# A language-model tower on one core: a sum of heads turned the other way, steps moved between engines, a last stage reordered

## The chip, the core and the metric

The kernel runs on one core of a Trainium2 chip. Five engines work side by side, each through its own instructions in the order in which they are written: TensorE (PE in the profile; its weight loads are PEld), VectorE (DVE), ScalarE (ACT), GpSimd (POOL) and SyncE (SP), which here mostly starts transfers. They wait for one another by semaphores. The metric is the device time of one execution in microseconds (us), the median of the runs shown.

## What is computed

32 sequences of 96 token numbers pass through three parts. In short:

```
# 1: embedding and an additive attention
x = emb[tokens]*sqrt(128) + pe
q, k, v = x@Wq+bq, x@Wk+bk, x@Wv+bv
s[b,i,j] = sum_d a[d] * tanh(q[b,i,d] + k[b,j,d])
x = layer_norm(x + softmax(s)@v@Wo + bo); h = layer_norm(x + relu(x@W1+bf1)@W2 + bf2)
# 2: causal attention with 8 heads of 128
h = h + attn(layernorm(h))
# 3: 64 experts, two for each token, and a shared one
t = _ln(layernorm(h)); idx, w = two largest of softmax(t@Wr@codebook.T/0.7), scaled to sum 1
hmoe = sum_k w_k*(silu(t@W1[e_k]+b1)@W2[e_k]+b2) + 0.25*(silu(t@Ws1+bs1)@Ws2+bs2)
out = h + (x3 + hmoe + silu(_ln(hmoe)@Wf1+bf1)@Wf2+bf2)      # x3 = layernorm(h)
```

The tanh is taken of 32 x 96 x 96 x 128 sums, 37.7 million: most of the first part's work.

## The kernel before, in words

**The tower.** Two sequences make a pair (192 tokens); 16 pairs. The program is written as rounds n = -1 to 21. Each engine has a `body(n)`, a list by hand of the steps of a round; `at(n, k, step)` runs the step for pair n - k if there is one, so in a full round some six pairs are in work, each in another part. `at_end` holds a step until the last pair. Nothing but this order and the semaphores decides what runs when.

The costly part is the tanh: for a pair VectorE forms eight blocks of sums with `add` (L941, 128x2304 each), ScalarE takes `tanh` of each (L688), TensorE weights and sums each with `score` (L1385, 24 instructions of 192 columns). The rest is fitted between. `x_rows` (VectorE, L954) forms a pair's embedding rows scaled plus `pe_rows`; `xs_turn`, `qk` and `queries` (L932) follow and allow the first `add` of that pair; `keep_x` (GpSimd, L555) keeps the rows with a bias. The layer norms (`stats`, `means`, `variance` on VectorE, `root` on GpSimd, L568 and L573) come four times in a pair: x1, x2, h0 and h1. `variance` adds eps; `root` raises to the power -1/2.

**Attention 2.** For a pair: `heads_g` (TensorE, L1498, 8 heads, 192 columns each), `scores` (L1519), `mask_max` and `exp2`, `inv_sums`, `normalise` (GpSimd, L578), `pr_turn` (L1526), `heads_m` (L1505, the probabilities times the rows: a mean for each head), `mean_copy` (ScalarE). Then the heads' sum: `o_begin` lays the residual h0 into PSUM as [96 tokens, 2 x 128], and four blocks of `attend2` (L1539) add the heads: the mean is the weight operand (96 columns), `vo` moves (128 columns), 8 instructions a block. `h1_stats` reads the sum. Then routing: `tn_turn`, `logits`, `route`, `chosen`, `one_hot` (VectorE, L1107: which of 64 experts), `both_hot`, `ranks` (L1560, L1118: the row's place at its expert), and `scatter_rows` (GpSimd, L620): four indirect DMAs put a pair's rows to their experts in DRAM. `cum_pair` (L595) carries the counts on; in the list it stands behind the scatters.

**The drain.** After the last pair has its scores, the rounds go on with fewer pairs until it is routed. Blocks of the shared expert (`shared1`, `shared2`, L1572 and L1589) are placed there. When all is counted, TensorE forms the rows for each expert (L1651, the "count"), a chain of small steps makes the tables, and the expert stage begins: 81 tiles of 128 rows, about 163 us, each with two products of TensorE.

**The last stage.** 12 blocks of 256 tokens. VectorE: `mixture` (weighted expert results into `hm`, statistics, variance, and the residual `rh` = hm + x), then it waits for GpSimd's root (L675), forms `fn` (L1349), and adds the `output` of block j - 2 (L1358). TensorE turns fn (L1743) and does two products (L1751, L1764), with ScalarE between.

## Time and profile before

| | us |
|---|---|
| median of 3 runs | 800.54 (799.36 to 802.94) |
| the profiled execution | 801.53 |
| its span in the trace | 799.5 |
| TensorE busy | 743.0 |
| VectorE busy | 611.6 |
| ScalarE busy | 615.2 |
| GpSimd busy | 366.5 |

By stage: start 0 to 12.6, where the first `add` begins; the filling of the pipeline to 88; the full rounds 88 to 490; the drain to 564; the expert stage 572 to 735; the last stage 747 to 799.5. A row of the timeline gives start, length, engine, line, operation, and in brackets the idle time before and what ended it. A float32 product of TensorE stands as two instructions in the trace. The chain of waits is followed back from the last instruction, each step to what released it.

### The profile page before, as it was taken

To read this page: it belongs to the slowest core of one execution; us is meant where nothing else is said; L and a number is where in the kernel's file an instruction comes from. 1 tells how busy PE (TensorE), PEld (TensorE's weight loads), DVE (VectorE), ACT (ScalarE), POOL (GpSimd) and SP (SyncE) were. 2 spreads that over 40 slices of the span, in tenths; PEclk is the share of its full clock that TensorE was granted. 3 is DMA by queue.
4 is the path that set the end of the run, shared out by engine and by line. 5 is a ranking of instruction groups with operands and counts; after the bars stand their busy time and mean duration, and the time that the engine had idled before them with its cause. 6 is when DMAs were issued, how large, how long until landed. Compare 5 with 4: busy or idle time off the path is not lost.

```text
span 799.5 us, 21390 instructions
## 1 busy us (share of the span) xinstructions
PE 743.0 (93%) x7238; PEld 594.1 (74%) x7238; DVE 611.6 (76%) x1634; ACT 615.2 (77%) x1455; POOL 366.5 (46%) x482
## 2 busy tenths in 40 slices
PE   2767999999999999999999999986899899999898
PEld 1454776776777777777777777765799899998787
DVE  4999899999999999999999996533434345433785
ACT  2787899999999999999999998763356465655454
POOL 3211234456465465465465455766047355554121
PEclk9999899999999999999999999997999999999999
DMA  2950000000000000000000000001599999993501
GB/s 79 251 120 6 5 5 7 12 17 14 12 16 14 12 16 17 12 16 17 12 17 16 12 12 12 17 20 31 175 384 375 402 395 365 346 359 119 168 29 39
DMA packets 50096, 78.99 MB, mean 99 GB/s; under 512 B 7428, under 2 KB 34203, under 8 KB 50000
## 3 DMA queue, kind: packets, MB, share of 16 engines
q1 hardware_dynamic: 33824, 65.01, 23.8%
q0 software_dynamic: 5664, 7.92, 3.7%
q10 hardware_dynamic: 10512, 4.83, 2.2%
q8 instruction: 56, 0.92, 0.5%
q14 instruction: 40, 0.33, 0.1%
HBM read 63.95 MB, written 15.92 MB: 100 GB/s over the span
## 4 chain that ended last, share of the span: by engine, by line
PE 75%; DVE 6%; issue 4%; SPq 4%; DMA 3%; ACT 2%; POOL 2%; POOLq 0%; DVEq 0%; ACTq 0%
PE b_s L1385 15%; PE b_o L1539 7%; PE big L1695 6%; PE big L1498 6%; PE big L1505 5%; PE big L1519 5%; DVE arena L941 4%; PE b_y L1482 3%; PE b_qk L1706 3%; PE b_s L1706 3%; PE big L1526 3%; PE big L1751 3%; DMA arena<-in_wpack 3%; PE big L1470 3%; PE b_s L1764 2%
## 5 line engine op out<-in xcount | busy, mean ns | idle before, releaser
L941 DVE TENSOR_TENSOR arena<-qT,b_qk 128x2304 f32<-128x2304 f32 x128 | 323.9, 2536 | 0.1
L688 ACT ACTIVATE arena<-arena 128x2304 f32<-128x2304 f32 x128 | 275.6, 2156 | 17.6 <-DVE arena L941 17.6
L1385 PE MATMUL b_s<-arena,apad 128*32 128x192 f32 x3072 | 155.7, 339 | 9.1 <-ACT arena L688 9.0
L1385 PEld LDWEIGHTS b_s<-arena,apad 128*32 128x32 f32 x3072 | 89.4, 112 | 78.6 <-issue 29.1
L849 ACT ACTIVATE act_h<-big,arena 128x128 f32<-128x128 f32 x324 | 92.4, 368 | 71.5 <-PE big L1695 71.5
L656 POOL DMA_INDIRECT eo_dram<-gT,toff x81 | 79.7, 984 | 95.0 <-DVE gT L1270 91.3
L1695 PE MATMUL big<-hbT,arena 128*128 128x128 f32 x648 | 87.0, 278 | 5.3 <-DMA arena<-in_wpack 3.9
L578 POOL TENSOR_TENSOR kept<-kept,rs 96x384 f32<-96x384 f32 x64 | 52.8, 824 | 78.1 <-DVE rs L1077 77.7
L750 ACT ACTIVATE kept<-big,mx 96x96 f32<-96x96 f32 x256 | 83.6, 354 | 1.7 <-DVE mx L1071 1.5
L1695 PEld LDWEIGHTS big<-hbT,arena 128*128 128x128 f32 x648 | 79.6, 193 | 6.2 <-issue 5.5
L1259 DVE TENSOR_SCALAR hbT<-b_t,cols 128x128 f32<-128x128 f32 x81 | 33.2, 409 | 61.5 <-PE b_t L1688 61.5
L620 POOL DMA_INDIRECT rows_dram<-rows_now,slots x64 | 62.2, 971 | 16.7 <-issue 15.7
L1539 PE MATMUL b_o<-kept,vv 128*96 128x128 f32 x512 | 66.4, 274 | 0.0
L1539 PEld LDWEIGHTS b_o<-kept,vv 128*96 128x96 f32 x512 | 59.2, 163 | 5.7 <-issue 5.3
L750 ACT ACTIVATION_READ_ACCUMULATOR kept<-big,mx 96x1 f32 x256 | 57.0, 222 | 0.0
L1505 PE MATMUL big<-prT,vv 96*128 96x384 f32 x128 | 53.7, 501 | 0.0
L1519 PE MATMUL big<-gT,xaT 128*96 128x384 f32 x128 | 52.4, 490 | 0.6 <-ACT gT L734 0.6
L1498 PE MATMUL big<-xaT,kept 128*128 128x192 f32 x256 | 52.4, 340 | 0.0
L1071 DVE TENSOR_REDUCE mx<-big 96x4 f32<-96x384 f32 x64 | 35.1, 549 | 15.1 <-PE big L1519 15.1
L1498 PEld LDWEIGHTS big<-xaT,kept 128*128 128x128 f32 x256 | 42.6, 195 | 5.1 <-issue 4.6
L555 POOL TENSOR_TENSOR res<-xs,v_bias 96x256 f32<-96x256 f32 x16 | 11.7, 730 | 72.5 <-DVE xs L954 58.2
L1706 PE MATMUL b_s<-arena,act_h 128*128 128x128 f32 x328 | 43.4, 275 | 0.3 <-ACT act_h L849 0.3
(226 smaller groups left out, 1441.8 us busy)
## 6 DMA issues: line engine op xcount, KB each, us to landing
arena<-in_wpack SPq DMA_DIRECT2D x81, 578.0 KB, 9.1
prT<-rows_dram ACTq DMA_DIRECT2D x73, 64.5 KB
rows_dram<-act_h SPq DMA_DIRECT2D x1, 4128.0 KB, 24.1
arena<-eo_dram SPq DMA_DIRECT2D x4, 512.0 KB, 7.1
x_dram<-res SPq DMA_DIRECT2D x16, 96.0 KB, 1.7
out<-of SPq DMA_DIRECT2D x12, 128.0 KB, 1.8
eo_dram<-gT,toff POOLq DMA_INDIRECT x81, 5.6
rows_dram<-rows_now,slots POOLq DMA_INDIRECT x64, 2.3
```

Source lines behind the costliest of these rows:

```text
L656: pool.indirect_dma_start(eo_dram, bass.IndirectOffsetOnAxis(ap=toff[:, r:r + 1].bitcast(U32), axis=0), eo[r], None, bounds_check=TOPK * T ...
L688: act.activation(v, v, ACT.Tanh).then_inc(s["tanh"], 1)
L750: last = act.activation(pr[:, h, :], bank(p, f"scores {k}")[0:N, j * N:(j + 1) * N], ACT.Exp, bias=mx2[:, h:h + 1], scale=-1.0, accum_out= ...
L849: last = act.activation(act_h[:, i, c * TILE:(c + 1) * TILE], big[i][:, c * TILE:(c + 1) * TILE], ACT.Silu, bias=wslot[:, slot, 2 * DFF + ...
L941: dve.tensor_tensor(ring[c % TRING].rearrange("p (x m n) -> p x m n", m=CQ, n=N), qv.unsqueeze(3).to_broadcast([D, SPLIT * QG, CQ, N]), kv ...
L1385: last = pe.matmul(b_s[32 * a:32 * a + 32, 0:SPLIT * N], apad[:, 31 - line:63 - line], t[:, :, a, m, :], start=(line == 0), stop=(line == ...
L1498: last = pe.matmul(dst[:, j * TN:(j + 1) * TN], mh[:, h * D:(h + 1) * D], xaT[:, :], start=True, stop=True)
L1505: pe.matmul(dst[:, 0:4 * N], xa[p % 2][:, k // 2, :], prT[:, 4 * k:4 * k + 4, :].rearrange("p a n -> p (a n)"), start=True, stop=True).the ...
L1519: pe.matmul(dst[0:N, 0:4 * N], xaT[:, g * N:(g + 1) * N], gT[:, h:h + 4, g * N:(g + 1) * N], start=False, stop=True).then_inc(s["s2"], 1)
L1539: last = pe.matmul(p_o[:, g, :], meanT[:, g * H + h, :], vo[:, h * D:(h + 1) * D], start=False, stop=(k == 3 and h == H - 1))
L1695: last = pe.matmul(big[of_ring(t, 2)][:, c * TILE:(c + 1) * TILE], wslot[:, slot, c * D:(c + 1) * D], hbT[:, of_ring(t, 2), :], start=True ...
L1706: last = pe.matmul([b_s, b_qk][of_ring(t, 2)][:, 0:D], act_h[:, of_ring(t, 2), c * TILE:(c + 1) * TILE], wslot[:, slot, DFF + c * D:DFF + ...
```

## The change

- **The heads' sum is turned.** `vo` becomes the weight operand (128 columns) and the means of both sequences move (192 columns): eight products, in two `attend2` halves of four heads, into `p_oT`, [128, 192]. VectorE copies it to `oT` (`oT_copy`), and `o_rows` lays h0 and two products with the identity, which turn it back, into `p_o`. `h1_stats` waits for that. The blocks of `scores` and `heads_m` are numbered anew, so that a half has the same four heads of both sequences. `o_begin` goes; h0 gets a second buffer.
- **To GpSimd go** `x_rows` (as a multiplication and an addition), the additions of eps (now in `root` and `roots_h1`), and `one_hot` (as four comparisons).
- **The orders of all engines are new.** On GpSimd `root h0` stands behind `root x2`, `x_rows` and the first scatters, and `cum_pair` ahead of the scatters. On TensorE `shared1 1` and `shared1 2`, `shared2 0` and `shared2 1` stand in the last round, behind the last pair's `ranks` of the round before.
- **In the last stage** GpSimd forms the residual (`last_residual`, ahead of the root), `hm` gets a second buffer, `rh` a fourth, and `output(j - 2)` stands ahead of `f_rows(j)`, the step that forms fn.
- Some semaphores are merged; the order of ScalarE's list is new as well, its steps are the same.

The diff, cut to its core (of VectorE's list the new order, of TensorE's list the new order with the lines that stay):

```diff
-RESIDUALS = 3
+RESIDUALS = 4
...
-        hm = sb("hm", [128, G, D])
+        hm = [sb(f"hm_{i}", [128, G, D]) for i in range(2)]
...
-        h0 = sb("h0", [N, G, D])
+        h0 = [sb(f"h0_{i}", [N, G, D]) for i in range(2)]
...
+        p_oT = b_o[:, G * D:G * D + TN]
...
+            def x_rows(p):
+                wait(pool, s["xs_t"], p)
+                if p < EARLY:
+                    pool.wait_ge(s[f"emb{p}"], 16 * G)
+                else:
+                    pool.wait_ge(s["emb2"], 16 * G * (p - (EARLY - 1)))
+                if p == 0:
+                    pool.wait_ge(s["ld_a"], 16 * 5)
+                wait(pool, s["kept"], p)
+                pool.tensor_scalar(xs[:, :, :], pair_of(res, p) if p < EARLY else emb[:, :, :],
+                                   float(np.float32(D) ** np.float32(0.5)), None, ALU.mult).then_inc(s["scaled"], 1)
+                pool.wait_ge(s["scaled"], p + 1)
+                pool.tensor_tensor(xs[:, :, :], xs[:, :, :], pe_rows[:, :].unsqueeze(1).to_broadcast([N, G, D]),
+                                   ALU.add).then_inc(s["xs"], 1)
+
...
             def root(p, n):
                 pool.wait_ge(s["var_" + n], p + 1)
+                pool.tensor_scalar(ve[n][:, :], mv[n][:, :, 1], EPS if n == "h0" else EPS_TOK, None, ALU.add)\
+                    .then_inc(s["ve_" + n], 1)
+                pool.wait_ge(s["ve_" + n], p + 1)
                 pool.tensor_tensor(rstd[n][:, :], ve[n][:, :], halves[:, 0:G], ALU.pow)\
                     .then_inc(s["rstd_" + n], 1)
             def roots_h1(p):
+                wait(pool, s["shift"], p)
                 pool.wait_ge(s["var_h1"], p + 1)
+                pool.tensor_scalar(ve_h[:, 0:G], mv["h1"][:, :, 1], EPS, None, ALU.add)
+                pool.tensor_scalar(ve_h[:, G:3 * G].rearrange("p (a g) -> p a g", g=G),
+                                   mv["h1"][:, :, 1].unsqueeze(1).to_broadcast([N, 2, G]),
+                                   1.0 + EPS, EPS * EPS, ALU.mult, ALU.add).then_inc(s["ve_h1"], 1)
+                pool.wait_ge(s["ve_h1"], p + 1)
                 pool.tensor_tensor(rstd_h[:, :], ve_h[:, :], halves[:, :], ALU.pow).then_inc(s["rstd_h1"], 1)
...
+            def one_hot(p):
+                wait(pool, s["slot"], p)
+                pool.wait_ge(s["topf"], p + 1)
+                for g in range(G):
+                    for k in range(TOPK):
+                        j = g * TOPK + k
+                        last = pool.tensor_scalar(oh[:, g, k, :], iota_e[0:N, :], of_pair(topf, p)[:, j:j + 1], None,
+                                                  ALU.is_equal)
+                last.then_inc(s["hot"], 1)
...
             def body(n):
+                at(n, 6, one_hot)
+                at(n, 6, both_hot)
+                at(n, 0, gather_emb, 0)
+                at(n, 3, root, "x1")
+                at(n, 6, counted)
+                at(n, 4, setup)
+                at(n, 6, keep_rows)
+                at(n, 6, residual)
+                at(n, 0, gather_emb, 1)
+                at(n, 4, normalise, 0)
+                at(n, 6, cum_pair)
+                at(n, 3, x1_bias)
+                at(n, 5, roots_h1)
+                at(n, 4, normalise, 1)
+                at(n, 1, keep_x)
+                at(n, 4, normalise, 2)
+                at(n, 4, normalise, 3)
+                at(n, 3, root, "x2")
+                at(n, 0, x_rows)
                 at(n, 6, scatter_rows, 0)
-                at(n, 0, gather_emb, 0)
-                at(n, 3, root, "x2")
-                at(n, 0, gather_emb, 1)
-                at(n, 4, normalise, 1)
-                at(n, 4, normalise, 2)
                 at(n, 3, root, "h0")
-                at(n, 4, normalise, 3)
                 at(n, 6, scatter_rows, 1)
-                at(n, 6, cum_pair)
-                at(n, 0, keep_x)
-                at(n, 2, root, "x1")
-                at(n, 5, both_hot)
-                at(n, 0, setup)
-                at(n, 5, counted)
-                at(n, 5, residual)
-                at(n, 2, x1_bias)
-                at(n, 5, keep_rows)
-                at(n, 3, normalise, 0)
-                at(n, 4, roots_h1)
...
+            def last_residual(j):
+                pool.wait_ge(s["mixed"], j + 1)
+                if j >= RESIDUALS:
+                    pool.wait_ge(s["of"], j - RESIDUALS + 1)
+                pool.tensor_tensor(rh[j % RESIDUALS], hm[j % 2][:, :, :],
+                                   xr[:, j, :].rearrange("p (g d) -> p g d", g=G), ALU.add).then_inc(s["rh"], 1)
+
...
+                last_residual(j)
...
-            def x_rows(p):
-                wait(dve, s["xs_t"], p)
-                wait(dve, s["kept"], p)
-                if p < EARLY:
-                    dve.wait_ge(s[f"emb{p}"], 16 * G)
-                else:
-                    dve.wait_ge(s["emb2"], 16 * G * (p - (EARLY - 1)))
-                dve.scalar_tensor_tensor(xs[:, :, :], pair_of(res, p) if p < EARLY else emb[:, :, :],
-                                         float(np.float32(D) ** np.float32(0.5)),
-                                         pe_rows[:, :].unsqueeze(1).to_broadcast([N, G, D]),
-                                         ALU.mult, ALU.add).then_inc(s["xs"], 1)
-
...
+                last.then_inc(s["var_" + n], 1)
+
...
+            def oT_copy(p):
+                wait(dve, s["o_rows"], p)
+                dve.wait_ge(s["att2"], 2 * p + 2)
+                dve.tensor_copy(oT[:, :], p_oT).then_inc(s["oT"], 1)
+
...
+                at(n, 0, add, 2)
+                at(n, 3, inv_sums, 2)
+                at(n, 4, h1_shift)
+                at(n, 2, x2_stats)
+                at(n, 1, softmax1_max)
+                at(n, 3, inv_sums, 3)
+                at(n, 2, means, "x2")
+                at(n, 0, add, 3)
+                at(n, 2, x2_rows)
+                at_end(n, 5, shared_rows, 0)
+                at(n, 1, p1T_copy)
+                at(n, 2, x2_norm)
+                at(n, 2, h0_stats)
+                at(n, 1, x1_sums)
+                at(n, 2, means, "h0")
+                at(n, 1, x1_rows)
+                at(n, 0, add, 4)
+                at(n, 1, x1_stats)
+                at(n, 2, xa_norm)
+                at(n, 4, route)
+                at(n, 0, add, 5)
+                at(n, 4, chosen)
+                at(n, 1, means, "x1")
+                at(n, 0, setup)
+                at(n, 0, add, 6)
+                at(n, 3, oT_copy)
+                at(n, 0, add, 7)
+                at(n, 2, mask_max, 0)
+                at(n, 1, x1_norm)
+                at(n, 4, ranks)
+                at(n, -1, queries)
+                at(n, 2, mask_max, 1)
+                at(n, 2, inv_sums, 0)
+                at(n, -1, add, 0)
+                at(n, 3, h1_stats)
+                at(n, -1, add, 1)
+                at_end(n, 5, shared_rows, 1)
+                at(n, 3, means, "h1")
+                at(n, 2, mask_max, 2)
+                at(n, 2, inv_sums, 1)
+                at(n, 2, mask_max, 3)
...
+                if j >= 2:
+                    dve.wait_ge(s["rh"], j - 1)
...
-                ch.link(dve.tensor_tensor(rh[j % RESIDUALS], hm[:, :, :], xr[:, j, :].rearrange("p (g d) -> p g d", g=G),
-                                          ALU.add))
+
...
+            def output(j):
+                dve.wait_ge(s["rh"], j + 1)
+                dve.wait_ge(s["f2"], j + 1)
+                if j:
+                    dve.wait_ge(s["out"], 16 * j)
+                for g in range(G):
+                    last = dve.tensor_tensor(of[:, g, :], [b_s, b_qk][g][:, 0:D], rh[j % RESIDUALS][:, g, :], ALU.add)
+                last.then_inc(s["of"], 1)
+
+            for j in range(NB):
+                mixture(j)
...
                 if j >= 2:
                     output(j - 2)
-            ch.wait()
+                f_rows(j)
...
-                pe.matmul(dst[:, 0:4 * N], xa[p % 2][:, k // 2, :],
+                pe.matmul(dst[:, 0:4 * N], xa[p % 2][:, k % 2, :],
...
-                g = k // 2
-                h = (k % 2) * 4
+                pe.wait_ge(*big_read(p, f"heads_g {2 * (k // 2)}"))
+                pe.wait_ge(*big_read(p, f"heads_g {2 * (k // 2) + 1}"))
+                g = k % 2
+                h = (k // 2) * 4
...
+            def attend2(p, half):
+                if half == 0:
+                    wait(pe, s["o_rows"], p)
+                for g in range(G):
+                    pe.wait_ge(*big_read(p, f"heads_m {G * half + g}"))
+                of_heads = meanT[:, half * G * 4:(half + 1) * G * 4, :].rearrange("p (g a) n -> p a g n", g=G)
+                for j in range(4):
+                    h = 4 * half + j
+                    last = pe.matmul(p_oT, vo[:, h * D:(h + 1) * D], of_heads[:, j, :, :],
+                                     start=(h == 0), stop=(h == H - 1))
+                last.then_inc(s["att2"], 1)
+
+            def o_rows(p):
                 wait(pe, s["tn"], p)
-                pe.wait_ge(s["h0_rows"], p + 1)
-                pe.matmul(b_o[0:N, 0:G * D], ident[0:N, 0:N], h0[:, :, :].rearrange("p g d -> p (g d)"),
-                          start=True, stop=False).then_inc(s["o_init"], 1)
-
-            def attend2(p, k):
-                pe.wait_ge(*big_read(p, f"heads_m {k}"))
-                g = k // 2
-                for h in range((k % 2) * 4, (k % 2) * 4 + 4):
-                    last = pe.matmul(p_o[:, g, :], meanT[:, g * H + h, :], vo[:, h * D:(h + 1) * D],
-                                     start=False, stop=(k == 3 and h == H - 1))
-                last.then_inc(s["att2"], 1)
+                pe.wait_ge(s["oT"], p + 1)
+                pe.matmul(b_o[0:N, 0:G * D], ident[0:N, 0:N], h0[p % 2][:, :, :].rearrange("p g d -> p (g d)"),
+                          start=True, stop=False)
+                for g in range(G):
+                    last = pe.matmul(p_o[:, g, :], oT[:, g * N:(g + 1) * N], ident[:, :], start=False, stop=(g == G - 1))
+                last.then_inc(s["o_rows"], 1)
...
             def body(n):
+                at(n, 3, ffn1, 1)
+                at(n, 2, score, 6)
+                at(n, 4, scores, 2)
+                at(n, 4, scores, 3)
+                at(n, 3, ffn2)
+                at_end(n, 6, shared2, 0)
+                at(n, 2, score, 7)
                 at(n, 4, pr_turn, 0)
+                at(n, 4, pr_turn, 1)
+                at(n, 4, pr_turn, 2)
+                at(n, 2, products)
+                at(n, 4, heads_m, 0)
                 at(n, 2, p1_turn)
+                at(n, 4, pr_turn, 3)
+                at_end(n, 5, shared1, 0)
+                at(n, 4, heads_m, 1)
                 at(n, 1, score, 0)
                 at(n, 2, attend1)
+                at(n, 5, tn_turn)
+                at(n, 1, setup)
+                at_end(n, 6, shared1, 1)
                 at(n, 1, score, 1)
+                at(n, 4, heads_m, 2)
+                at(n, 4, heads_m, 3)
+                at(n, 5, logits)
+                at(n, 4, attend2, 0)
                 at(n, 1, score, 2)
+                at(n, 3, xa_turn)
+                at(n, 1, v_rows)
+                at(n, 4, attend2, 1)
+                at(n, 1, score, 3)
+                at(n, 3, heads_g, 0)
+                at(n, 0, xs_turn)
                 at_end(n, 6, shared2, 1)
                 at(n, 3, heads_g, 1)
                 at(n, 3, heads_g, 2)
+                at(n, 1, score, 4)
+                at(n, 3, scores, 0)
+                at(n, 5, ranks)
+                at(n, 3, heads_g, 3)
+                at(n, 0, qk)
+                at(n, 3, scores, 1)
                 at(n, 2, x1_turn)
+                at(n, 4, o_rows)
+                at(n, 1, score, 5)
+                at_end(n, 6, shared1, 2)
                 at(n, 2, ffn1, 0)
```

## Rows read from the trace of the kernel before

**Rows 1.** Busy by stretch: length; PE, PEld, DVE, ACT, POOL; granted clock; DMA.
```profile
241.59:272.14 30.55, 30.55 (x338) 22.30 (x342) 30.45 (x73) 29.82 (x66) 16.90 (x23) 1.00 0.06 15
541.00:560.00 19.00, 12.75 (x59) 10.35 (x58) 6.83 (x45) 5.84 (x12) 12.06 (x17) 0.71 0.12 32
```

**Rows 2.** Chain of waits in a round: start, us, engine, tile, line, instructions.
```profile
292.40 0.88 PE b_o L1539 x8
...
296.49 1.33 PE big L1498 x8
```

**Rows 3.** Timeline of the start: start, us, engine, line, operation, out<-in, [idle before].
```profile
8.81 0.42 DVE L954 SCALAR_TENSOR_TENSOR xs<-res,pe_rows 96x256 f32<-96x256 f32 x1 [3.21 <-DMA res<-in_L_tok_emb,eidx]
...
10.39 0.97 POOL L539 MEMSET act_h<- 128x1024 f32 x1
...
12.56 12.41 DVE L941 TENSOR_TENSOR arena<-qT,b_qk 128x2304 f32<-128x2304 f32 x5
```

**Rows 4.** Timeline of VectorE: `queries` at both ends of twelve rounds.
```profile
87.45 0.42 DVE L932 TENSOR_SCALAR qT<-b_qk,bqk 128x192 f32<-128x192 f32 x1 [0.17 <-PE b_qk L1408]
...
454.60 0.40 DVE L932 TENSOR_SCALAR qT<-b_qk,bqk 128x192 f32<-128x192 f32 x1
```

**Rows 5.** Timeline of the drain.
```profile
540.71 1.06 PE L1539 MATMUL b_o<-kept,vv 128*96 128x128 f32 x8
...
541.88 0.48 DVE L984 BATCH_NORM_STATS2 stat_h<-b_o 96x6 f32<-96x128 f32 x2
...
550.98 0.31 PE L1560 MATMUL b_y<-ohs,tri_h 96*96 96x128 bf16 x1 [1.17 <-POOL cums L604]
...
553.24 0.84 ACT L789 ACTIVATE act_h<-big,cols 128x256 f32<-128x256 f32 x2 [3.38 <-PE b_s L1589]
...
554.71 1.66 PE L1572 MATMUL big<-hall,ws 128*128 128x256 f32 x4
...
558.38 0.24 PE L1651 MATMUL b_t<-cums,ones_h 96*113 96x64 bf16 x1 [2.02 <-POOL cums L595]
```

**Rows 6.** Chain of waits in the last stage.
```profile
752.92 1.73 PE big L1751 x8
...
756.65 1.73 PE big L1751 x8
...
788.93 1.73 PE big L1751 x8
...
793.02 1.73 PE big L1751 x8
```

**Rows 7.** Timeline of VectorE in the last stage, one block.
```profile
768.37 0.42 DVE L1340 TENSOR_TENSOR vv<-hm,res 128x256 f32<-128x256 f32 x1
...
769.38 0.60 DVE L1349 TENSOR_SCALAR gT<-hm,fmv,frstd 128x128 f32<-128x128 f32 x2 [0.59 <-POOL frstd L675]
...
769.90 0.28 DVE L1358 TENSOR_TENSOR of<-b_s,vv 128x128 f32<-128x128 f32 x1
```

**Rows 8.** Timeline of VectorE in the round of the first stretch.
```profile
263.30 0.42 DVE L954 SCALAR_TENSOR_TENSOR xs<-emb,pe_rows 96x256 f32<-96x256 f32 x1
...
263.64 0.16 DVE L1002 TENSOR_SCALAR ve_x<-mv_x 96x2 f32<-96x2 f32 x1
...
266.69 0.42 DVE L1107 TENSOR_TENSOR oh<-iota_e,topf 96x256 f32<-96x256 f32 x1
...
271.32 0.40 DVE L932 TENSOR_SCALAR qT<-b_qk,bqk 128x192 f32<-128x192 f32 x1
```

**Rows 9.** Groups of GpSimd in that round: busy us, mean ns, idle before, releaser.
```profile
L620 POOL DMA_INDIRECT rows_dram<-rows_now,slots x4 | 3.9, 981 | 1.0 <-issue 1.0
L568 POOL TENSOR_TENSOR rstd_x<-ve_x,halves 96x2 f32<-96x2 f32 x2 | 1.5, 734 | 0.0
L584 POOL TENSOR_SCALAR res<-tn,grow,mv_h 96x128 f32<-96x128 f32 x2 | 0.9, 445 | 0.0
L555 POOL TENSOR_TENSOR res<-xs,v_bias 96x256 f32<-96x256 f32 x1 | 0.7, 734 | 2.6 <-DVE xs L954 2.6
```

247 lines of the change are left out of this document (74 added, 173 removed), and 10 rows, old and new, of tables (BIG_ORDER, s).

## The prediction

> **What bounds the kernel now.** I read the busy time by stretch first. In a round of the tower (one pair of sequences enters, others are in later steps) TensorE is busy 30.55 us of 30.55, VectorE 30.45, ScalarE 29.82, GpSimd only 16.90 [rows 1]. So three engines are full together, and what is taken from one is worth at most its distance to the next. Then the chain of waits: through the rounds it runs over TensorE blocks that touch one another at their usual price [rows 2], so the round is TensorE's own length. Then the timeline at four places: the start, where VectorE's sums stand back to back [rows 3]; the rounds' length, from `queries` 87.45 to `queries` 454.60, 12 rounds of 30.60 [rows 4]; the drain after the last score, where one pair's latency is the path and TensorE's granted clock averages 0.71 [rows 1, 5]; and the last stage, 12 blocks, whose period is 3.73 us at first and 4.09 at the end [rows 6, 7]. The expert stage between them isn't touched: it moves as a whole with the tables that open it.
>
> **The change part by part.**
>
> *Heads' values (PE L1539).* Before: 4 blocks of 8 instructions for a pair, 0.88 us a block [rows 2], 3.52 us. After: 8 heads with 192 moving columns and 128 weight columns, two instructions in the trace for each, the shape of `heads_g`, of which 8 instructions take 1.33 [rows 2]: 2 x 1.33 = 2.66. The turn back adds 4 instructions of 128 columns, 4 x 0.88/8 = 0.44; laying h0 down costs the same, only later. Net 2.66 + 0.44 - 3.52 = -0.42 us a round, so TensorE's round would be 30.13.
>
> *VectorE.* `x_rows` starts at 263.30 and lets the next one start at 263.64: 0.34. `one_hot` has the same 0.42 us length, so 0.34 too. An instruction overlaps the next by some 0.08, so each of the five variance additions (0.16 long) occupies 0.08 [rows 8]. Removed 0.34 + 0.34 + 0.40 = 1.08. Added: the copy of the turned sum out of PSUM, 128x192, priced as `queries`, 0.40 long [rows 8], 0.32 net. VectorE's round becomes 30.45 - 0.76 = 29.69.
>
> *ScalarE* keeps its 29.82 of work. So the new round lies between 30.13 and 30.55. The copy must stand between the last `attend2` and `o_rows`: TensorE has two `score` blocks, `scores 0` and `scores 1` and all of `heads_g` to do there, of which `heads_g` alone, 1.33 [rows 2], hides copy and handover in a full round; without that cover a round would pay some 0.6. I take 0.35 of the 0.42, because ScalarE has only 0.3 left for waits where it now has 0.7. 12 x -0.35 = **-4.2**; ends 0 and 12 x -0.42 = -5.0.
>
> *GpSimd* gets, in a round: the scaling of the rows as two instructions (0.89 as twice the 96x128 one, and 0.73), four comparisons of 96x64 (each between the 0.16 that VectorE needs for 96x2 and GpSimd's own 0.445 for 96x128, say 0.3), five small additions (the same ends, say 0.2) [rows 8, 9]. 0.89 + 0.73 + 1.2 + 1.0 = 3.8, so 20.7 of 30: hidden as a sum. As a queue it is the second rival.
>
> The Trainium skill (GPSIMD Engine Reference, 4.1 Engine selection) speaks against moving elementwise work to this engine, about twice as slow with two inputs; the trace agrees, 0.73 against 0.42 for 96x256 [rows 8, 9]. By that rule alone the moved work would lose 1.75 times what VectorE gains; by the rows GpSimd has 13 us a round idle to lose it in, so the sum counts nothing.
>
> *The start.* Today VectorE forms pair 0's rows at 8.81, done by 9.23, as soon as they land; the first sum starts at 12.56. On GpSimd this stands behind its opening fills, of which the last starts at 10.39 and takes 0.97 [rows 3]. So it begins at 11.36 and ends 0.89 + 0.73 and two handovers (0.1 each) later, 13.2 instead of 9.23: +3.9. VectorE's sums follow one another from there, so nothing hides it. Up to `queries` 87.45 VectorE is the bound and saves its `x_rows` three times, 1.0: **+2.9**. Ends: +1.8 if first scores and tables catch up another microsecond, +4.4 if the scaling costs 0.5 more.
>
> *The drain.* Of the last pair every step is on the path. Today `h1_stats` starts 1.17 us after the last `attend2` block's start, 541.88 against 540.71, that is 0.27 after its end [rows 5]. After: copy 0.40, then 0.1, h0 and turn back 8 x 0.11 = 0.88, 0.27 again: +1.65. Variance additions on GpSimd in front of the power: +0.3. One-hot as four comparisons there: 1.2 against 0.42 with a shorter handover, +0.7. Three rounds of the drain save 0.42 each, -1.25. Then the count of rows per expert, which opens the tables. Today it runs 7.4 us after the ranks (558.38 against 550.98), and its last 2.02 are a wait for GpSimd's `cum_pair` [rows 5], which stands behind four row scatters; in the new order it stands in front of them. That wait goes. What is late next is TensorE itself: `shared1 1`, `shared1 2` used to run before the ranks and now run behind them, so five blocks (`shared2 0`, `shared1 1`, `shared2 1`, `shared1 2`, `shared1 3`) precede the count instead of three, and `shared2 1` waits about 1.2 for ScalarE's activation of the block before (0.84 and two handovers). A block costs 1.7 at the lower clock [rows 5] and 0.9 at full. With three at the lower clock and two at full: 5.1 + 1.8 + 1.2 + 0.3 = 8.4, +1.0. Sum 1.65 + 0.3 + 0.7 - 1.25 + 1.0 = **+2.4**. All five at the lower clock: +4.0; all at full, 6.0 us: 0.0; and the other steps of the drain are reordered too, which I can't sum, so I go down to -2.5.
>
> The Trainium skill (TensorE: Matmul & The Clock Gate, Part 1) says that this engine's clock falls after idling and returns with sustained work. The trace agrees: 0.71 granted in the stretch where waits pile up [rows 1]. By that rule the five dense blocks could bring it back sooner, and the sum would lose up to 2.4; no run here shows where.
>
> *The last stage.* In the steady part VectorE repeats with 4.09 and is the bound. From its residual's start, 768.37, to `fn`, 769.38, pass 1.01: 0.42 of residual and 0.59 of waiting for GpSimd's root [rows 7]. The root sets that stretch, with or without a residual in it. After, `output` (two instructions of 0.28, overlapping by 0.08 and followed by one that overlaps too, 0.40) fills it, and its own place behind `fn` is gone: 4.09 - 0.40 = 3.69. The residual, on GpSimd some 0.73 for 256 columns [rows 9], starts when the mixture is written, about 0.9 before the root is asked for, so it is done in time. What is late next is TensorE, which needs 3.73, the period that it shows before VectorE falls behind. Between 752.92 and 793.02 ten periods take 40.1 [rows 6]; at 3.73 they take 37.3: **-2.7**, with a tenth for the first ones. Ends -2.9 and -1.0 (if the residual delays the root by 0.2 each time). Merged semaphores, the second buffers for h0 and hm: nothing.
>
> Sum: +2.9 - 4.2 + 2.4 - 2.7 = -1.6 us. The profiled execution took 801.53 (span 799.5), so 799.9; it lies 0.99 above the median of its runs, 800.54. On that median: 798.9, a change of 0.2%.
>
> **The rivals.**
>
> *Faster: the drain doesn't pay.* If TensorE's clock is back for the blocks behind the ranks, the freed `cum_pair` counts in full (6.0 us, not 8.4), and if the reordered scores and copies of the last pairs save some 2 us more, and rounds win the whole 0.42 (-5.0): 2.9 - 5.0 - 2.0 - 2.7 = -6.8, 793.7. For it: 2.02 of waiting for `cum_pair`. Against: the clock was low here.
>
> *Slower: GpSimd's queue becomes what VectorE waits for.* The place is `root h0`, which now stands behind `root x2`, `x_rows` and two scatters: 0.2 + 0.1 + 0.73, 0.89 + 0.73 + 0.1, 2 x (0.98 + 0.3), and 1.0 for itself: 6.3 us, with 0.73 for a power and 0.3 of issue for a scatter [rows 9], and it starts some 0.7 late, behind `normalise 3`. VectorE does two sums between its x2 means and `xa_norm`, 2.48 each as five take 12.41 [rows 3], and eight small steps that I estimate at 2.7 together: 7.7 us. So 0.7 is left, and another 0.4 of VectorE's slack against TensorE. It decides from the point where the moved work costs 1.1 us more than I gave it; at 1.7 more, each round loses 0.6 against 30.13, so that 12 rounds cost +2 instead of -4.2: 805.
>
> *No gain in the rounds.* ScalarE's 29.82 and as much waiting as today give 30.55 again: 2.9 + 0 + 2.4 - 2.7 = +2.6, 803.1.
>
> **How the numbers follow.** Forecast 798.9, chance 0.45 (796 to 802); faster rival 0.29; no gain in the rounds 0.10; slower rival 0.16. A measurement here can tell about 0.5%, 4.0 us, from no change: 796.5 to 804.5. Faster by more: 0.29 and 0.03 of the forecast's edge, 0.32; slower by more: 0.16 and 0.03 of the no-gain case, 0.19; within: 0.49. The range takes in both outer rivals with a little beyond: 792 to 806.5.
>
> **What would show it.** First sum near 16.5 instead of 12.56; `queries` 30.2 us apart; `attend2` as two blocks of 1.33; VectorE idle for a few tenths in each round, none of it before `xa_norm`; last stage at 3.73 with TensorE not waiting for VectorE; the count about 8.4 after the last ranks. I am wrong if rounds are not 30.1 to 30.3, if VectorE waits for `rstd_h0`, or if the expert stage opens over 2 us from today's time.

## The result: 0.7% slower, and the profile after

The changed kernel takes 806.48 us (median of 7, 802.15 to 809.34) against 802.5 for the kernel before (median of 7): ratio 1.0066, 95% interval 1.0035 to 1.0097. A second comparison gave 805.76 against 801.08, 1.0079 (1.0053 to 1.0106). Forecast were 798.9 and no measurable change; the loss of 4.0 to 4.7 us is small and real.

The profiled execution is the quickest of its seven (802.15, span 800.3), so I compare stretches of the traces, not totals. Where a half-clock stretch of TensorE falls in the filling of the pipeline differs between executions of the same code there: two kernels that are alike up to the fourth `queries` (after and attend_early, below) have this step at 88.75 and 91.17. "Half clock" is a granted clock of 0.5, the lower of the two levels; "last ranks" are those of the last pair, "count" is L1651 in before and L1679 in after.

| stretch | forecast | after less before |
|---|---|---|
| first sum of VectorE | +3.9 | +3.89 (16.45) |
| fourth `queries` | +2.9 | +1.30 (88.75) |
| twelve rounds | -4.2 | -0.75 |
| from there to the last ranks | +1.4 | +7.08 |
| ranks to count | +1.0 | -0.05 |
| count to the last stage's first output | 0 | -4.6 |
| the outputs of the last stage | -2.7 | -2.2 |

The -4.6 is for the most part not the change's. 1.9 of it lies in the expert stage, where before's trace has a half-clock stretch (624 to 628) and after's has none. 1.2 lies between that stage and the last stage's first product, 12.3 in before and 11.2 in after; the trace of turned_alone (below), with before's code there, has 11.2 too. But 1.3 lies between the last stage's first product and its first output, 6.16 in before and 4.85 in after. turned_alone, with before's last stage and full clock, also has 6.16, so I count these 1.3 with the last stage. Without the other 3.1 the stretches come to +3.8, close to what the medians show.

VectorE's timeline in the kernel after, start of the first sums and both ends of the twelve rounds (12 rounds of 30.53, but 30.67 in the steady ones; the first takes only 29.02. Before had 30.60 on the mean [rows 4], 30.55 in its steady ones):

```profile
16.45 9.95 DVE L990 TENSOR_TENSOR arena<-qT,b_qk 128x2304 f32<-128x2304 f32 x4
...
88.75 0.42 DVE L981 TENSOR_SCALAR qT<-b_qk,bqk 128x192 f32<-128x192 f32 x1
...
455.15 0.42 DVE L981 TENSOR_SCALAR qT<-b_qk,bqk 128x192 f32<-128x192 f32 x1
```

Busy time of the kernel after by stretch (columns as in [rows 1]): a full round, and 10 us of the drain in which the last pair's means and heads' sum are formed:

```profile
301.81:332.48 30.67, 30.34 (x324) 22.14 (x323) 30.21 (x67) 29.85 (x67) 21.45 (x35) 1.00 0.06 15
534.70:544.94 10.24, 10.24 (x31) 7.59 (x30) 1.02 (x7) 3.95 (x9) 5.94 (x9) 0.51 0.07 19
```

No engine is full in the round now. The chain of waits in a round shows who sets it: VectorE's `topf` (the chosen experts), then GpSimd from there to the ranks, 5.5 us. Between the one-hot rows and `counted`, which writes the `cums` that TensorE's ranks wait for, stand `gather_emb` (1.09) and the x1 root. TensorE stands 0.24 us a round in front of the ranks:

```profile
417.09 0.17 DVE topf L1131
...
417.43 1.71 POOL oh L630 x4
...
419.29 0.44 POOL ohs L637
419.73 0.35 issue
420.08 1.09 POOL emb L523
...
421.57 0.20 POOL rstd_x L589
421.77 0.52 issue
422.28 0.30 POOL cums L641
422.59 0.14 issue
422.72 0.23 PE b_y L1590
```

VectorE's timeline in the drain of the kernel after, at `xa_norm` of the last pair. Before waits for nothing at this step; after waits 1.04 in the pair before the last, and here 2.13, for the root h0:

```profile
521.44 0.60 DVE L1088 TENSOR_SCALAR vv<-h,mv_h,rstd_h 96x128 f32<-96x128 f32 x2 [2.13 <-POOL rstd_h L589]
```

From the last pair's `normalise` to the end of `attend2`, GpSimd's and TensorE's timelines of the kernel before:

```profile
535.02 0.82 POOL L578 TENSOR_TENSOR kept<-kept,rs 96x384 f32<-96x384 f32 x1 [0.46 <-DVE rs L1077]
...
539.07 0.81 PE L1505 MATMUL big<-prT,vv 96*128 96x384 f32 x2
539.72 1.04 PE L1539 MATMUL b_o<-kept,vv 128*96 128x128 f32 x8
```

GpSimd's `normalise` 1 to 3 in the kernel after:

```profile
532.27 2.39 POOL L605 TENSOR_TENSOR kept<-kept,rs 96x384 f32<-96x384 f32 x3
```

TensorE's timeline in the drain of the kernel after:

```profile
533.23 0.51 PE L1549 MATMUL big<-ident,kept 96*96 96x96 f32 x4 [1.88 <-POOL kept L605]
...
537.87 2.82 PE L1528 MATMUL big<-prT,vv 96*128 96x384 f32 x4
...
541.07 4.62 PE L1560 MATMUL b_o<-vv,kept 128*128 128x192 f32 x16
...
546.30 0.64 PE L1567 MATMUL b_o<-h,ident 96*96 96x256 f32 x2 [0.50 <-DVE oT L1105]
...
558.61 0.31 PE L1590 MATMUL b_y<-ohs,tri_h 96*96 96x128 bf16 x1 [4.33 <-POOL cums L641]
...
565.96 0.19 PE L1679 MATMUL b_t<-cums,ones_h 96*113 96x64 bf16 x1
```

VectorE's two means of the h1 statistics, in the kernel before and in the kernel after:

```profile
542.46 0.24 DVE L993 BATCH_NORM_AGGREGATE mv_h<-stat_h 96x2 f32<-96x6 f32 x2
...
548.37 0.24 DVE L1030 BATCH_NORM_AGGREGATE mv_h<-stat_h 96x2 f32<-96x6 f32 x2 [0.46 <-DVE stat_h L1021]
```

Against [rows 5] and the rows of before above: the last pair is 1.2 us ahead of before at the end of its last `normalise` (534.66 against 535.84). Then the clock is at half from 534.5 to 544.7 (in before's drain it fell first at 545.7). The means cost 2.0 more. From the last mean to the end of `attend2` pass 5.0 instead of 1.9, 3.1 more: in both kernels 16 instructions of `attend2` stand behind the last mean, but they last 4.62 instead of 2.1, and before does half of them while it waits for the last mean's copy. The copy and the turn back cost 1.6, eps on GpSimd 0.4, the one-hot rows 1.35. VectorE's means come 0.46 behind their statistics instead of 0.10, which is another 0.4; the runs don't show why. Together -1.2 + 2.0 + 3.1 + 1.6 + 0.4 + 0.4 + 1.35 = 7.65, and the ranks stand at 558.61 against 550.98.

The last stage's chain in the kernel after: TensorE's product L1779 (before: L1751) every 3.73 us to the end, where [rows 6] came to 4.09.

```profile
782.50 1.73 PE big L1779 x8
...
786.24 1.73 PE big L1779 x8
```

### The profile page after: what moved, and what is told of

The parts are those of the page before. It is cut to its first block and busy times, and to the rows that moved or that the text cites. A ratio compares the mean times of both kernels' runs of the same rounds, so it can differ in the third digit from the quotient of the medians.

```text
span 800.3 us, 21184 instructions
## 1 busy us (share of the span) xinstructions
PE 735.0 (92%) x7046; PEld 587.8 (73%) x7046; DVE 604.6 (76%) x1526; ACT 614.3 (77%) x1455; POOL 445.3 (56%) x670
## 5 line engine op out<-in xcount | busy, mean ns | idle before, releaser
L1408 PE MATMUL b_s<-arena,apad 128*32 128x192 f32 x3072 | 157.7, 341 | 7.4 <-ACT arena L735 7.4
L1408 PEld LDWEIGHTS b_s<-arena,apad 128*32 128x32 f32 x3072 | 89.9, 113 | 55.6 <-issue 24.3
L797 ACT ACTIVATION_READ_ACCUMULATOR kept<-big,mx 96x1 f32 x256 | 59.9, 234 | 0.0
L1560 PE MATMUL b_o<-vv,kept 128*128 128x192 f32 x256 | 49.4, 338 | 0.0
L630 POOL TENSOR_SCALAR oh<-iota_e,topf 96x64 f32<-96x64 f32 x64 | 27.2, 438 | 38.1 <-DVE topf L1131 38.0
L1094 DVE TENSOR_REDUCE mx<-big 96x4 f32<-96x384 f32 x64 | 34.7, 542 | 14.6 <-PE big L1542 14.5
L1521 PEld LDWEIGHTS big<-xaT,kept 128*128 128x128 f32 x256 | 40.7, 189 | 4.9 <-issue 4.6
L1560 PEld LDWEIGHTS b_o<-vv,kept 128*128 128x128 f32 x256 | 42.8, 197 | 0.3
```

What stands on the lines that cost most here:

```text
L797: last = act.activation(pr[:, h, :], bank(p, f"scores {k}")[0:N, j * N:(j + 1) * N], ACT.Exp, bias=mx2[:, h:h + 1], scale=-1.0, accum_out= ...
L1408: last = pe.matmul(b_s[32 * a:32 * a + 32, 0:SPLIT * N], apad[:, 31 - line:63 - line], t[:, :, a, m, :], start=(line == 0), stop=(line == ...
L1521: last = pe.matmul(dst[:, j * TN:(j + 1) * TN], mh[:, h * D:(h + 1) * D], xaT[:, :], start=True, stop=True)
L1560: last = pe.matmul(p_oT, vo[:, h * D:(h + 1) * D], of_heads[:, j, :, :], start=(h == 0), stop=(h == H - 1))
```

## The experiments

**The last stage alone, and the turned sum alone**, each put into the kernel before.

```diff
 last_stage_alone: mixture, f_rows, output, last_residual, hm x2, RESIDUALS = 4
 turned_alone:     attend2(half), oT_copy, o_rows, h0 x2, the numbering of scores and heads_m
```

> The kernel before with only the last stage's part of the change (residual on GpSimd, two buffers of hm, a fourth of rh, output ahead of f_rows). Prediction's term: period 3.73 us throughout, 2.2 to 2.7 us less than before, ratio about 0.997. If the gain of the last stage in the changed kernel came from its clock instead, the period stays above 3.9 and the total moves by under 1 us.

Measured: 797.64 against 801.08, ratio 0.9961 (0.9945 to 0.9977); outputs 3.73 apart throughout (754.51 to 791.84 in ten periods). The mechanism stands, and of the two parts tried alone this is the one that wins.

> The kernel before with the turned sum of heads alone (two halves of attend2, the copy, the turn back; two buffers of h0), everything else and every order kept as far as it goes. Prediction's term: TensorE's round 30.13 instead of 30.55; with VectorE now 30.45 + 0.32 = 30.77 the round is VectorE's: 30.5 to 30.8, so no gain without the steps moved off VectorE, and a drain longer by 1.5 to 3 us: total 0 to 5 us slower than before. If VectorE's overlaps hide the copy, the round falls to 30.2 and the total comes out 1 to 3 us faster.

Measured: 818.14 against 800.52, ratio 1.0228 (1.0206 to 1.0251): 17.6 us, where 5 were expected at most. The twelve rounds, of 31.40, cost 8.8 of it, and from the last sum to the ranks pass 78.69 instead of 70.23. VectorE is busy 31.07 in a round:

```profile
305.83:337.24 31.41, 30.46 (x324) 22.15 (x323) 31.07 (x74) 30.05 (x67) 16.86 (x23) 1.00 0.06 15
```

The expectation had 30.5 to 30.8; VectorE is busy 0.62 more than in [rows 1], where the copy was put at 0.32. No engine is full in these rounds. In before's order the turned sum loses without the steps that leave VectorE; whether another order would do, no run here shows.

**Who sets the round.** In the kernel after, one line of GpSimd's list is moved:

```diff
                 at(n, 6, both_hot)
+                at(n, 6, counted)
                 at(n, 0, gather_emb, 0)
                 at(n, 3, root, "x1")
-                at(n, 6, counted)
```

> The changed kernel, unchanged, for a second look at where a usual execution of it loses against before (ratio 1.005 or so expected). If the loss sits in the drain: first sum of VectorE near 16.45 again, rounds of 30.67 again, last ranks 6 to 10 us later than in before's trace (550.98), and stretches of half clock in the drain. If instead the rounds lose in a usual execution, queries will be more than 30.9 apart.

> The changed kernel with one line moved: on GpSimd the step counted stands right behind both_hot, ahead of gather_emb 0 and root x1. Theory (the round is set by GpSimd's chain from the chosen experts to the ranks, for which TensorE waits 0.25 us a round): that wait goes, rounds fall from 30.67 to 30.3 to 30.45, 12 rounds give 2.5 to 4.5 us, and the drain some 1 us more (two rounds in which the ranks stood behind these steps). Rival (ScalarE with 29.85 of work and its two waits for TensorE, 0.82 a round, sets it): rounds stay within 0.05 of 30.67, the wait turns up elsewhere, and the total moves by under 1 us.

Measured: after_again as told above (rounds of 30.70, ranks at 558.73, half clock from 534.5 to 544.7). counted_first 801.24 against 801.08, ratio 1.0008 (0.9991 to 1.0024), 4.5 us less than after_again on the same chip; rounds of 30.38:

```profile
300.70:331.10 30.40, 30.16 (x324) 22.22 (x323) 30.26 (x68) 29.97 (x66) 21.56 (x34) 1.00 0.06 15
```

TensorE's 30.16 is close to the forecast's 30.13. So the handover to the ranks had eaten 0.29 a round; the twelve rounds take 363.33, 3.8 less than before's 367.15. The rival of the expectation, ScalarE, falls: it has the same work and less waiting. VectorE isn't where the forecast had it: 30.26, not 29.69. And a wait for GpSimd is left, at another place: TensorE stands 0.24 in front of `pr_turn`, for a `normalise` queued behind `roots_h1`, which itself waits for VectorE's mean. The timelines of TensorE and GpSimd in counted_first:

```profile
250.93 0.51 PE L1549 MATMUL big<-ident,kept 96*96 96x96 f32 x4 [0.24 <-POOL kept L605]
...
246.53 0.21 POOL L595 TENSOR_SCALAR ve_h<-mv_h 96x2 f32<-96x2 f32 x1 [3.57 <-DVE mv_h L1030]
```

TensorE's work and its wait at this step make the round: 30.14 and 0.24 here, 30.14 and 0.11 in x_rows_back (30.25), 30.20 and 0.46 in one_hot_back (30.66), both below.

**VectorE's missing half microsecond.** VectorE's timeline in the kernel after, in a full round and in one in which no new pair enters:

```profile
316.35 0.91 DVE L1075 SCALAR_TENSOR_TENSOR h<-xg,rstd_x,row_beta 96x128 f32<-96x128 f32 x2
...
469.25 0.59 DVE L1075 SCALAR_TENSOR_TENSOR h<-xg,rstd_x,row_beta 96x128 f32<-96x128 f32 x2
```

GpSimd's timeline at the first of the two:

```profile
316.11 0.72 POOL L566 TENSOR_TENSOR xs<-xs,pe_rows 96x256 f32<-96x256 f32 x1
```

For the twelve pairs beside whose `h` GpSimd's addition of `x_rows` runs, `h` takes 0.90 or 0.91; for the other four, 0.59 to 0.64. The runs that try this, and the one-hot rows, start from the kernel "together" (below), with the first sum at 14.59, rounds of 30.38 and a median of 791.69; x_rows_back has VectorE's old `x_rows` again, one_hot_back its old `one_hot`.

> The kernel of together (rounds 30.38, first sum 14.59, median 791.69) with the embedding rows back on VectorE as one instruction. In the trace after, VectorE's step h (its second layer norm's last two instructions, each with two operands in SBUF) takes 0.91 us in every round in which GpSimd's addition of x_rows runs beside it, and 0.59 in the two rounds without. Theory (moving x_rows took 0.34 off VectorE and put 0.31 on): h falls to 0.6, VectorE's round stays within 0.1 of 30.25, rounds stay at 30.3 to 30.45; the first sum comes at 12.4 to 13; the total falls by 1 to 2.5 us. Rival (the move had bought VectorE its 0.34): rounds 30.6 to 30.75, the total 1 to 3 us more.

Measured: 789.89, ratio 0.9871 (0.984 to 0.9903); first sum at 12.58; rounds of 30.25, the twelve together 362.18. VectorE's timeline in it:

```profile
312.55 0.60 DVE L1073 SCALAR_TENSOR_TENSOR h<-xg,rstd_x,row_beta 96x128 f32<-96x128 f32 x2
```

Its busy time in a round:

```profile
298.44:328.69 30.25, 30.13 (x323) 22.19 (x322) 30.11 (x69) 29.79 (x67) 20.00 (x32) 1.00 0.06 15
```

VectorE does an instruction more in a round and is busy 0.12 less than in "together" (30.23). `h` gives back 0.31, and `x1_norm` 0.15 (0.59 instead of 0.74); what had slowed `x1_norm` no run shows. So the move of `x_rows` brought nothing to the rounds, it cost 0.13 each. The first sum comes 2.0 earlier, the fourth `queries` 0.9 later (87.50 against 86.59, with other half-clock stretches before it), so this trace can't say what the start won. The total is 1.8 under together's, but the intervals of the two ratios overlap.

> The kernel of together with the one-hot rows of all pairs back on VectorE. If VectorE (30.25 of 30.38) sets the round with TensorE: rounds 30.5 to 30.75, 12 rounds cost 2 to 4 us against 1.3 us won in the drain: total 0.5 to 3 us more than together. If only ScalarE and TensorE set it: rounds 30.38, total 1 to 1.5 us less.

Measured: 793.89, ratio 0.9914 (0.9882 to 0.9947), against 791.69 and 789.89; rounds of 30.66, VectorE busy 30.48 of 30.65. Moving the one-hot rows was worth 0.28 a round, 3.4 over the twelve: that part of the change holds, once `counted` follows them at once. In the drain the move costs: from the last sum to the ranks one_hot_back takes 73.00, together 74.53.

**The drain: order or clock.** First against the kernel after:

```diff
+                at_end(n, 4, attend2, PAIRS - 1, 0)
                 at(n, 4, heads_m, 2)
                 at(n, 4, heads_m, 3)
                 at(n, 5, logits)
-                at(n, 4, attend2, 0)
+                if n - 4 != PAIRS - 1:
+                    at(n, 4, attend2, 0)
```

> The changed kernel, but for the last pair alone the first half of attend2 stands ahead of heads_m 2 and heads_m 3 on TensorE, so that it runs while these wait for their copies. Theory (the order in the drain left both halves, 16 instructions, behind the last mean): the last ranks come 1.3 us earlier at full clock, 2.2 at half, and the total falls by as much. Rival (only the half clock in that stretch costs): the ranks move by under 0.5 us.

Measured: 809.86 against 801.08, ratio 1.0112 (1.0088 to 1.0136). Up to the last pair's `normalise` its trace runs 2.4 us behind after_again's (the filling), at the ranks 5.1: the edit loses 2.7. 1.0 of it is lost up to the end of `attend2`: TensorE now waits 1.07 for the second copy in front of the early half, in a stretch that it had filled without a gap. The other 1.8 come behind it: the `logits` of the pair before are 3.6 later, so GpSimd counts that pair later, and `o_rows` stands behind its ranks. TensorE's timeline in attend_early:

```profile
542.02 2.90 PE L1560 MATMUL b_o<-vv,kept 128*128 128x192 f32 x8 [1.07 <-ACT vv L788]
...
551.28 0.23 PE L1590 MATMUL b_y<-ohs,tri_h 96*96 96x128 bf16 x1 [2.19 <-POOL cums L641]
```

My theory of the order falls for this place; whether the early half would win behind `logits`, no run shows. Next, against counted_first: fill the idle time, or take it away.

```diff
 fill:        at(n, 4, pr_turn, 0)
+             if n - 4 == PAIRS - 1:
+                 keep_busy(8)       # ident by ident into b_qk
 roots_late:  normalise 1, normalise 2, then roots_h1 (last pair's round only)
 root_first:  root h0, scatter_rows 0, scatter_rows 1
```

> The kernel of counted_first (ranks 554.29, count 563.71, median 801.24), with eight products added that nobody reads (TensorE, identity by identity into the idle bank of the queries, 16 instructions, 1.8 us) for the last pair alone, where TensorE stands idle for 1.89 us between pr_turn 0 and pr_turn 1. They lie in that idle time. Theory (the idle time drops TensorE's clock to half for the products of heads_m and attend2 behind it): the granted clock stays at 1.0 there, the ranks come 2 to 4 us earlier, the total falls by as much. Rival (the clock falls anyway, or the path there isn't TensorE's): ranks within 0.5 us of 554.3.

Measured: TensorE's timeline in fill: the same 16 instructions of `attend2` take 2.82 (3.55 in counted_first, where the clock rose under way, 4.62 in after).

```profile
530.49 1.98 PE L1627 MATMUL b_qk<-ident 128*128 128x128 f32 x16
...
535.53 1.56 PE L1528 MATMUL big<-prT,vv 96*128 96x384 f32 x4
...
537.24 2.82 PE L1560 MATMUL b_o<-vv,kept 128*128 128x192 f32 x16
...
541.73 0.23 PE L1590 MATMUL b_y<-ohs,tri_h 96*96 96x128 bf16 x1 [1.68 <-POOL cums L641]
```

The busy time of that stretch, granted clock 1.00 (third number from the end):

```profile
531.60:541.00 9.40, 8.11 (x50) 6.22 (x49) 2.42 (x12) 5.62 (x19) 8.11 (x12) 1.00 0.08 21
```

From the last sum to the ranks 74.05 us instead of 76.32: 2.3 won in the trace. The total doesn't show it (800.69, ratio 0.9998, 0.9978 to 1.0018, against 801.24 and 1.0008); executions differ by as much in the filling, where this trace lost 2.25. A half clock that begins between 528 and 537 stands in all eight traces of the changed kernel and its variants that leave this idle time; in the seven that fill it (fill, ranks_late, together and four built on it) the first one of the drain begins at 542.6 to 547.8. The last row shows the next wait: `o_rows` is queued behind ranks that GpSimd hasn't fed.

> The kernel of fill, and in the round of the last pair's second attention the ranks of the pair before stand behind o_rows on TensorE. In fill TensorE waits 1.67 us for GpSimd in front of these ranks, with o_rows queued behind them. Theory: that is why the 3.25 us that fill won up to the copy of the turned sum were 2.3 at the ranks; h1_stats comes 1 to 1.6 us earlier, the total falls by as much. Rival (VectorE takes h1_stats only behind its own ranks step): under 0.4 us.

Measured: 799.47, ratio 0.9991 (0.9972 to 1.0011), 1.2 under fill, which is within the noise; from the last sum to the ranks 73.90, 0.15 under fill. The wait before `o_rows` went (0.61 for the copy is left) and came back as a longer one for `tn`, 4.88 instead of 4.01. The rival was right.

> The kernel of counted_first, but in the one round in which the last pair is normalised GpSimd's roots_h1 of the pair before stands behind normalise 1 and 2. It takes away what TensorE waits for (1.89 us) instead of filling it. If GpSimd's queue is the path there: ranks 1.5 us earlier at the same clock, 4 to 5 us earlier if the clock stays up as well. If roots_h1 delayed only the pair before last, which isn't the path: within 0.5 us.

Measured: 803.89, ratio 1.0046 (1.0028 to 1.0063); from the last sum to the ranks 78.21, 1.9 longer. `normalise 3` now waits behind `roots_h1`, and VectorE's sums for it behind `h1_shift`, which needs `roots_h1`. Both expectations missed this.

> The kernel of counted_first with root h0 ahead of the first two scatters on GpSimd. The slower rival's place: scatters (1.3 us each) in front of the root. In the full rounds VectorE doesn't wait for it, so rounds stay at 30.38; in the drain, where the chain runs over these scatters twice, two pairs gain up to 2.6 us each: xa_norm of the last pair 2 to 5 us earlier, the total 1 to 4 us less. If VectorE's other work hides it there too: under 0.5 us.

Measured: 806.8, ratio 1.0089 (1.007 to 1.0108). Rounds stay at 30.38. VectorE's wait for the root h0 of the last pair falls from 2.13 to 1.24, but counted from the last sum its `x1_norm` comes 1.6 later and the ranks 4.8: the scatters, moved back, now delay the next one-hot rows, and TensorE stands 1.71 and 2.34 us before the ranks with `heads_g`, `scores` and `o_rows` queued behind. In both orders tried, GpSimd's queue holds the drain.

**The start and the count**, against counted_first:

```diff
 start_early: x_rows(0) ahead of GpSimd's fills
 shared_back, in TensorE's list:
                 at_end(n, 5, shared1, 0)
+                at_end(n, 5, shared1, 1)      # then tn_turn
                 at(n, 5, logits)
+                at_end(n, 5, shared1, 2)
+                at_end(n, 5, shared2, 0)
+                at_end(n, 5, shared2, 1)      # then ranks
```

> The kernel of counted_first with pair 0's embedding rows formed on GpSimd ahead of its fills instead of behind them. First sum 2 to 2.5 us earlier (16.3 to 14). The prediction took the delay of the start to last to the end (less 1.0); then the total falls by 2 to 2.5 us. Rival, from the trace after (the fourth queries are only 1.3 us late): something later sets the pace, and the total falls by under 1 us.

Measured: 801.79 (796.12 to 803.87), ratio 1.0009 (0.999 to 1.0028): no difference that these runs can show; its trace has the first sum at 14.64 and the fourth `queries` at 89.65. In "together" the gain is kept: first sum 14.59, fourth `queries` 86.59 and the last 449.85, against 16.49, 88.55 and 451.79 in shared_back with the same rounds: 1.9 to the last `queries`. Single traces differ by 3 there, so the means say more: nine traces with the first sum at 16.3 to 16.5 have their fourth `queries` at 89.9 on the mean (88.55 to 91.50), four with 14.6 at 88.3 (86.59 to 89.65). Of 1.8 at the first sum 1.6 are left.

> The kernel of counted_first, with the blocks of the shared expert put back ahead of the last ranks: shared1 0 and 1 in front of the last tn_turn, shared1 2, shared2 0 and shared2 1 behind the last logits, where TensorE stands idle for 4.0 and 4.6 us. In counted_first the count comes 9.4 us behind the ranks (554.29 to 563.71), because five blocks precede it, some at half clock. Theory (TensorE's blocks behind the ranks hold the count, the step that the prediction named): the count comes 2 to 4 us behind the ranks, the ranks move by under 1 us, the expert stage opens 4 to 7 us earlier, the total falls by 4 to 7 us. Rival (the row scatters, whose last one starts 6.3 us behind the ranks, or the tables hold it): under 2 us.

Measured: 794.82 against 801.16, ratio 0.9938 (0.9913 to 0.9962); counted_first had 801.24, so 6.4 less. TensorE's timeline in shared_back:

```profile
553.74 0.23 PE L1590 MATMUL b_y<-ohs,tri_h 96*96 96x128 bf16 x1 [0.41 <-POOL cums L641]
...
555.69 0.24 PE L1679 MATMUL b_t<-cums,ones_h 96*113 96x64 bf16 x1 [0.75 <-POOL cums L622]
```

The count stands 1.95 behind the ranks, not 9.4. The change had freed `cum_pair` and given the time away again to blocks of the shared expert. This is the largest single gain of all the runs.

> All four edits, fill, shared_back, start_early and ranks_late, on counted_first. If they add up: 5 to 10 us less than counted_first, 791 to 796, ratio to before 0.988 to 0.995, and so faster than both kernels. If they hide one another (a later table or a scatter holds what is won): 797 to 800.

Measured: 791.69 against 801.16, ratio 0.989 (0.9871 to 0.9908), as expected if the four edits add up.

> The kernel of together with the one-hot rows of the last pair alone formed by VectorE, as before the change. The prediction gave GpSimd's four comparisons 0.7 us more on the path of the drain; the trace after shows 1.35 (7.64 late behind the one-hot step, 6.29 ahead of it). If that is what they cost: last ranks and count 1.2 to 1.5 us earlier, the total 1 to 1.5 us less. If the scatters hold the expert stage by now: the count earlier, the total within 0.5.

Measured: 792.81, ratio 0.9901 (0.9872 to 0.993), no gain over together. Counted from `topf`, the last pair's one-hot rows are done 1.7 us earlier, the ranks aren't: TensorE's blocks put in front of them now end last.

> x_rows_back and one_hot_last in one kernel. If both hold and add up: 2 to 4 us less than together, 788 to 790.

Measured: 789.32 against 800.62, ratio 0.9855 (0.9823 to 0.9887): faster than the kernel before by over 1%, and than the changed one by more. It is 2.4 under together and 0.6 under x_rows_back; the latter is within the noise.

## Why the prediction was wrong, step by step

The two steps that failed are the rounds, which brought 3.5 us less than forecast, and the drain up to the ranks, which cost 5.7 more. 806.48 lies just inside the stated range, 792 to 806.5, by luck: both rivals up there had another cause. The one without a gain in the rounds, 803.1, blamed ScalarE, which counted_first refutes; the slower one, 805, put its loss into the full rounds behind `root h0`, and there VectorE never waits for it. The prediction's own signs of being wrong did show: rounds of 30.67, VectorE waiting for `rstd_h0` in the drain, and an expert stage that opens 7.3 later.

- *Heads' values.* TensorE's work was forecast at 30.13 a round; x_rows_back shows 30.13, counted_first 30.16. Right.
- *The rounds, -4.2.* Measured -0.75. The step that failed is "hidden as a sum": GpSimd was costed by its 13 us of idle time, and as a queue only at `root h0`. The wait came at another place of the same queue, at `counted` behind the one-hot rows, `gather_emb` and the x1 root; with `counted` moved the rounds give -3.8, with `x_rows` back as well -5.0. The slower rival had the mechanism. Its place, `root h0`, holds VectorE only in the drain (1.04 and 2.13).
- *VectorE.* Forecast 29.69, measured 30.26. Of the 0.34 that `x_rows` gave back, 0.31 came back on `h`: `h` and GpSimd's addition each have two operands in SBUF, and they run at the same moment. The trace of before couldn't show this, since its GpSimd hardly met that step. The Trainium skill (SBUF — State Buffer, SBUF: two separate sides) states that a VectorE instruction with two SBUF inputs and a GpSimd instruction that reads SBUF exclude one another for a whole instruction; the trace agrees in that `h` went from 0.59 to 0.91 while GpSimd's addition kept its 0.72. This was the rule that spoke against the change, and I had weighed another. With `x_rows` back on VectorE, its 30.11 is near the forecast's own terms, 29.69 + 0.34 = 30.03. So the move of `x_rows` explains nearly all of the miss: 0.31 by this meeting, 0.15 on `x1_norm`, of which the cause stays open.
- *The start.* +3.9 at the first sum was right. The +2.9 at the fourth `queries` can't be judged by this trace's +1.30: the nine traces with this start have 88.55 to 91.50 there, and before's code 87.45 and 88.13 (last_stage_alone). By the means that is +2.2, inside the stated ends of 1.8 and 4.4. A delay at the start does count, as start_early's comparison shows.
- *The drain, +2.4.* Measured +7.0: +7.1 up to the ranks, where +1.4 was forecast, and -0.05 for the count. The turn back was right (1.65 forecast, 1.6), though the gap before `h1_stats`, put at 0.27, is 0.11 in [rows 5]: its block lasts 1.06. The time saved ahead of it was right (1.25, 1.2), and eps (0.3, 0.4). Mis-sized were the one-hot rows (0.7, measured 1.35: comparisons of 0.43, not 0.3). Left out were two things between `normalise` and the copy, 5.1 together; the prediction has only that the other steps are reordered too. One is the clock, 4.0 by the rows: it was at half for the means (2.0) and for the way from the last mean to the end of `attend2` (5.0 instead of fill's 3.0), behind an idle time of 1.88 for `normalise` behind `roots_h1`. I had the clock fall behind the ranks only, as in [rows 1]. The other is the turned sum itself, 1.1: for the same way fill takes 3.0 at full clock, before 1.9. That the clock falls there with this idle time and stays up where it is filled, the fifteen traces show; how much of the total it costs, they don't, since only the trace shows fill's gain.
- *The count, +1.0.* Measured -0.05: five blocks took 7.35, not 8.4. The nine traces with five blocks there have 7.3 to 9.9, as the clock falls, so 8.4 was a fair middle. The step was right in kind, and shared_back shows what it gave away: the count 7.5 us nearer to the ranks than in counted_first.
- *The last stage, -2.7.* Measured -2.2 in the outputs and -1.3 in front of the first one, -3.5 together; alone 3.4 on the medians (interval 1.8 to 4.4). The mechanism and the period were right, the sum was a little small.

## What to carry to other kernels

When three engines are full and a fourth is idle, cost a step moved to the fourth by its place in that engine's queue: follow each moved step to the first instruction elsewhere that waits for what is queued behind it, at the steady round and again at the drain, where the same order has other steps missing. In a drain put independent work where an engine would stand idle ahead of the path's dense part, not behind the last result that the next stage needs. And check what the helper engine reads at the moment when the full engine reads.

## What the runs showed of the hardware

- An idle time of TensorE of 1.9 us (in roots_late 2.7 in three pieces) at the last pair's `normalise` came with half clock at the dense work around it in eight traces out of eight; eight products that nobody reads, put into it, kept the clock at 1.00 there. In pieces both came about: the kernel before idled there for 0.57, 1.11 and 0.58 and kept its clock, turned_alone for 1.18, 1.11 and 1.02 and fell to half at 546.7. What decides it, these runs don't show.
- GpSimd's comparison of 96x64 takes 0.43 to 0.44, as long as its 96x128 scaling (0.445), for half the elements.
- VectorE's `h` and GpSimd's addition of `x_rows`, each with two SBUF operands, cost VectorE 0.31 a meeting, and GpSimd nothing (0.72 to 0.73 with and without).
